# GpSimd normalises the tiles, VectorE keeps their moments

## The reference

```python
def _layernorm(x, axis=-1, eps=1e-05):
    m = jnp.mean(x, axis=axis, keepdims=True)
    v = jnp.var(x, axis=axis, keepdims=True)
    return (x - m) / jnp.sqrt(v + eps)

x = x + self_attention(_layernorm(x))     # layer 0: causal, 16 heads of 16
x = x + cross_attention(_layernorm(x))    # 77 context rows
x = x + experts(_layernorm(x))            # 8 linear experts, top 2
x = x + recurrence(_layernorm(x))         # layer 1: h = tanh(xt + h @ Wh.T + b), 1024 steps
x = x + cross_attention(_layernorm(x))
x = x + gated_experts(_layernorm(x))      # 16 experts in groups, top 4, and a shared one
```

## Time and profile before

| | |
|---|---|
| median of 3 runs | 1412.26 us (1410.08 to 1412.88) |
| the profiled execution, its own time | 1410.35 us |
| its span, first to last instruction | 1408.3 us |
| PE busy | 1353.7 us (96%) |
| DVE busy | 849.8 us (60%) |
| ACT busy | 630.1 us (45%) |
| POOL busy | 39.4 us (3%) |

### The profile page before, as it was taken

How to read it: one execution, slowest core, us unless ns; L and a number is a source line. 1 busy time by engine, 2 the same in 40 slices (tenths; PEclk the granted TensorE clock), 3 DMA queues, 4 the chain that set the end, 5 groups by cost and what they waited for, 6 DMA issues and landing times.

```text
span 1408.3 us, 48623 instructions
## 1 busy us (share of the span) xinstructions
PE 1353.7 (96%) x19876; PEld 918.5 (65%) x19876; DVE 849.8 (60%) x2678; ACT 630.1 (45%) x2842; POOL 39.4 (3%) x60
## 2 busy tenths in 40 slices
PE   4798979999999999999999999999999999999998
PEld 2455436777756777776577777766667776765654
DVE  6757774268775225979661225758555565447585
ACT  2163304833524784253248876553253435433422
POOL 2000000000000000000000000000000000000000
PEclk9899989999999999999999999989999999989999
DMA  5746100021000002110000003310000200001000
GB/s 139 122 124 128 37 1 3 3 50 16 3 2 3 3 3 34 40 34 3 2 3 3 3 3 108 81 30 2 2 2 3 55 3 3 17 3 39 2 16 15
DMA packets 45471, 40.20 MB, mean 29 GB/s; under 512 B 9723, under 2 KB 44486, under 8 KB 45254
## 3 DMA queue, kind: packets, MB, share of 16 engines
q1 hardware_dynamic: 42662, 35.53, 11.1%
q10 hardware_dynamic: 2592, 1.57, 0.9%
HBM read 25.81 MB, written 10.80 MB: 26 GB/s over the span
## 4 chain that ended last, share of the span: by engine, by line
PE 90%; DVE 5%; DMA 1%; ACT 1%; issue 1%; SPq 0%; DVEq 0%; ACTq 0%
PE b L515 23%; PE b L1654 9%; PE b L534 8%; PE b L1431 6%; PE b L1023 6%; PE b L994 5%; PE b L1722 5%; PE b L939 4%; PE b L696 3%; DVE mx L948 3%; PE b L1300 3%; PE b L1275 2%; PE b L744 2%; PE b L459 2%; PE b L651 2%; PE b L501 1%
## 5 line engine op out<-in xcount | busy, mean ns | idle before, releaser
L515 PEld LDWEIGHTS b<-hp,whp 128*128 128x128 f16 x12276 | 472.1, 96 | 255.1 <-ACT hp L560 168.6
L515 PE MATMUL b<-hp,whp 128*128 128x2 f16 x12276 | 532.5, 165 | 1.0
L566 DVE TENSOR_TENSOR hp<-hist,hp 128x4 f16<-128x4 f32 x1023 | 164.5, 161 | 405.6 <-ACT hist L561 394.9
L560 ACT ACTIVATE hp<-b 128x4 f16<-128x4 f32 x1024 | 178.0, 174 | 442.8 <-PE b L515 430.2
L948 DVE TENSOR_REDUCE mx<-b 128x1 f32<-128x512 f32 (+3 forms) x304 | 189.9, 652 | 0.5 <-PE b L939 0.3
L1008 ACT ACTIVATE vp<-b 128x512 f32<-128x512 f32 x288 | 171.7, 603 | 17.7 <-PE b L997 9.8
L561 ACT ACTIVATE hist<-b 128x4 f32<-128x4 f32 x1024 | 177.2, 173 | 0.0
L534 PE MATMUL b<-whp 128*128 128x512 f16 (+6 forms) x608 | 162.1, 342 | 0.0
L1654 PE MATMUL b<-vp,heads 128*128 128x512 f16 x576 | 160.5, 380 | 0.0
L939 PE MATMUL b<-heads 128*128 128x512 f16 (+3 forms) x384 | 113.1, 333 | 5.8 <-DVE mx L948 2.8
L1431 PE MATMUL b<-we,xT 128*128 128x512 f16 x384 | 106.0, 383 | 0.0
(11 more groups left out here) (220 smaller groups left out, 1620.7 us busy)
## 6 DMA issues: line engine op xcount, KB each, us to landing
x_qs<-qx_scr SPq DMA_DIRECT2D x42, 128.0 KB
qx_scr<-xq_pair SPq DMA_DIRECT2D x16, 256.0 KB, 2.1
heads<-q_scr SPq DMA_DIRECT2D x24, 128.0 KB, 5.0
heads<-k_scr SPq DMA_DIRECT2D x36, 64.0 KB, 2.8
x<-in_x SPq DMA_DIRECT2D x8, 256.0 KB, 6.7
q_scr<-tail SPq DMA_DIRECT2D x8, 256.0 KB, 2.3
k_scr<-tail SPq DMA_DIRECT2D x8, 256.0 KB, 2.3
x_qs<-in_L_ffn_We SPq DMA_DIRECT2D x2, 1024.0 KB, 6.2
```

Of the source, the lines that this page charges most:

```text
L515: return pe.matmul(self.z(t)[:, m], self.w.whp[:, a, k, m * P:(m + 1) * P], self.g.hp16[:, (t - 1) % 2, part, k, :], start=False, stop=Tru ...
L560: act.activation(self.g.hp16[:, t % 2, 0], self.z(t), ACT.Tanh, scale=1 / LIFT).then_inc(self.s["hi_ready"], 1)
```

## The change

`normalise` goes from DVE's list to POOL's, with the same instruction, waits and signal. Its cost in the plan becomes 0.75 (it was 0.49), and what follows it sees its signal after 0.15 in the plan (it was 0.06). Moments, power and transposition are as before; the planner makes a new order for all engines from the changed costs.

```diff
         st.add("pool", name + "_power", self.power, n // 2, 0.75, lambda h: rank(2 * h) + 0.4)
-        st.add("v", name + "_normalise", self.normalise, n, 0.49, r(0.5))
+        st.add("pool", name + "_normalise", self.normalise, n, 0.75, r(0.5))
...
-    def normalise(self, v, i):
+    def normalise(self, pool, i):
         t = tile_of(i)[3]
-        v.wait_ge(self.s["power"], i // 2 + 1)
+        pool.wait_ge(self.s["power"], i // 2 + 1)
         if i >= self.ring:
-            v.wait_ge(self.s["turned"], i - self.ring + 1)
-        v.tensor_scalar(self.xn[:, i % self.ring], self.g.x[:, t, :], self.g.mv[:, t, 0:1], self.g.rs[:, t:t + 1],
+            pool.wait_ge(self.s["turned"], i - self.ring + 1)
+        pool.tensor_scalar(self.xn[:, i % self.ring], self.g.x[:, t, :], self.g.mv[:, t, 0:1], self.g.rs[:, t:t + 1],
                         ALU.subtract, ALU.mult).then_inc(self.s["xn"], 1)
```

## The result

| | before | after |
|---|---|---|
| median of 20 runs each | 1410.84 us | 1430.7 us |
| profiled execution, own time | 1410.35 | 1434.52 |
| mean granted clock, profiled execution | 0.977 | 0.963 |
| recurrence, first to last tanh (L560) | 220.2 to 1272.7 | 225.1 to 1296.7 |
| PE idle over the span | 54.6 | 71.0 |

The ratio is 1.0128, with an interval of 1.0104 to 1.0152. I had predicted 1407 us, range 1399 to 1421. The ratios, the medians and the means from here on leave out the slow runs, those over 1.5% above the fastest of the same kernel (two of the 20 after, and one each of before, e5 and e9); without them the median after is 1430.1.

A forecast was written before the change was run, and what follows sets the result against it. DVE was taken to bound about a fifth of the kernel, PE with the recurrence's steps the rest. Terms of 6.6 us faster, zero and 2.0 slower made 4.6 faster: predicted 1407 us, range 1399 to 1421.

The forecast's parts named there:

- the price of POOL's instruction: One normalisation on POOL was taken at 0.55 us, range 0.41 to 1.23, below the planned 0.75.
- fourth rival: Single-buffer groups: above 0.75 us every round is later than planned; at 1.0 us PE loses 5 us, giving 1414; chance 0.08.
- Term 1: Relief of DVE in its full stretches, 32 tiles at 0.33 us: ceiling 10.6 us, taken as 6.6 us faster.
- first rival: Whole ceiling and more: lighter DVE lets the plan drop up to 15.7 us of idle matmuls; 1401, to 1396.6; chance 0.18.
- that shrinking: Sign for the forecast: PE's idle matmuls of L534 fall from 162 us by 5 to 15.
- The halving of the gain beside the recurrence: For 24 tiles beside the recurrence, half the freed DVE time was counted: 4.0 us, bounds 0 and 7.9.
- Term 2: Latency of a tile group: six waiting places 1.5 us slower, shorter DVE queue at the end 1.5 faster, together zero.
- The part that I expected at the end: In n6 of chunk 3 POOL starts the third tile sooner than busy DVE: 1.5 us faster, bounds 0 and 2.7.
- Term 3: POOL and DVE share a port: normalisations beside the recurrence delay DVE's subtraction, 2.0 us slower, bounds 0 and 9.4.
- third rival: POOL's normalisation holds up the recurrence's subtraction L566 for its whole length: slower, 1418 at 0.8 us, 1422 at 0.90; chance 0.21.
- second rival: Nothing moves: PE and the recurrence close up, a new order loses elsewhere what it gains; 1412 us; chance 0.13.
- The signs: Expected: DVE about 38 us lighter, POOL about 90 busy. Wrong if POOL's instruction takes 0.8, steps lengthen or idle matmuls don't shrink.

The follow-up runs named there:

- e5: The changed kernel with a plain copy on POOL in place of the normalisation, mean and factor left out, same order; 1394.7 us, ratio 0.9876.
- e9: The kernel before, normalisation still on DVE, with the factor left out (one arithmetic step); 1409.1 us, ratio 0.9979.
- m1: The kernel before, with nine forms of POOL instruction run twice each after the last store, other engines idle; one execution, no ratio.
- e7: The changed kernel with idle matmuls of 1024 columns before each transposition L459 once the recurrence runs; 1432.2 us, ratio 1.0142.
- e2: The changed kernel's order kept on every engine, but DVE executes the normalisations; 1415.7 us, ratio 1.0017 against before.
- e6: The changed kernel with one arithmetic step on POOL (mean subtracted, factor left out), same order; 1401.0 us, ratio 0.9940.
- e4: The kernel before, plus an unused instruction of the same form on POOL beside each DVE normalisation; 1416.7 us, ratio 1.0045.
- e1: The order of the kernel before kept on every engine, but POOL executes the normalisations; 1456.8 us, ratio 1.0320.
- e10: Against before: tiles of the five single-buffer sublayers split, 128 columns each on POOL and DVE, first sublayer on DVE; 1424.6 us, ratio 1.0081.

## Why the prediction was wrong, step by step

**The step that failed is the price of POOL's instruction.** I chose 0.55 from the row of the same shape; it is 1.24. With it fell what I built on it: "the order has room for it, and PE is not late". The plan had 0.75, and PE was late 42 times, for 20.6 us. The value of the upper bound, 1.23 from a power stretched by a neighbour, was right by accident. The two selections of the earlier trace rows gave 1.2 ns a column; a tensor_scalar with two steps has 3.3. A selection is no measure for arithmetic, and no row of the trace before was a good one; the power's 0.69 for two elements, which I quoted, lay above the price that I chose for 256. The price was unknown between 0.41 and 1.23; I put the forecast, with 0.40 of the chance, near its lower end, and worked out no rival beyond 1.0.

The Trainium skill (GPSIMD Engine Reference, section Performance versus the Vector engine) has elementwise work with two inputs at about twice VectorE's time. For two inputs m1 agrees roughly: 0.72 us on POOL, where DVE's addition of the same shape (L705, one of whose inputs lies in PSUM) took 0.42. For the normalisation, one input and two steps, the factor is three, 1.22 to 0.41; the measurement decides, and my estimate of 0.56 by that page fell with the price.

**The mechanism was the fourth rival's**, with 0.08 the least of my chances: above 0.75 every round of a single buffer is later than planned. I had priced it at one tile in four and 5 us, at d = 1.0. At 1.24 PE waited for 42 of the 80 tiles, 20.6 us (of it 12.2 in 34 waits beside the recurrence). And I had no term for the clock: of the difference of 16.9 us between the means, 9.0 are there at equal clock and 7.9 go with the lower one (0.0084 times 943). How much of that clock is due to the waits is not shown: e7 brought it back by filling them, but e2, with the same order and without them, has 0.9692 too. In e6, at 0.94, PE still waited for POOL 20 times, but 8.7 us in all, and that is less than the relief of DVE is worth. So the sign turns between 0.94 and 1.24.

**Term 1 was too small, and had the instruction been as short as I priced it, the sign would have held.** At equal clock e5 against e2, one order and one plan, differs by 10.5 us for a POOL instruction as long as DVE's own; the ceiling was 10.6 and I took 6.6. The medians differ by 21 us, as e5 has the higher clock too. Against before, e5 at 1394.7 and e6 at 1401.0 gain 17 and 10 us, which is the size of the first rival (1401, down to 1396.6); a right price alone would have left my 4.6 too small. The idle matmuls shrank by 15.8 us even in the kernel that lost (162.1 to 146.3), near the first rival's 15.7. I had named that shrinking as a sign that the forecast works; it is none, because it is made by the plan and not by the chip: e2 has the same 519 of them. The halving of the gain beside the recurrence (no second reduction fits into a step) is the likely weak step in this term; no run tests it by itself.

**Term 2** had six places at 0.14 and 0.1 for the later signal; with 1.24 the same places cost 0.83 each. The start of the recurrence shows it, 225.1 against e2's 219.8 with the same order. The part that I expected at the end seemed to come: from the end of the last variances (L439) to the last transposition of n6 it was 1348.84 - 1343.01 = 5.8 us and is now 1373.31 - 1368.58 = 4.7:

```profile
1368.41 0.17 DVE L439 TENSOR_SCALAR ve<-mv 128x2 f32<-128x2 f32 x1
...
1373.31 0.41 PE L459 MATMUL b<-ident,n_xn 128*128 128x128 f32 x2 [0.52 <-DVE vp L1528]
```

But e2, where DVE still normalises, has 1340.96 - 1337.75 = 3.2 us there:

```profile
1337.58 0.17 DVE L444 TENSOR_SCALAR ve<-mv 128x2 f32<-128x2 f32 x1
...
1340.96 0.38 PE L464 MATMUL b<-ident,n_xn 128*128 128x128 f32 x2
```

So the new order brought 2.6 us and POOL cost 1.5 of them; that my sign came true was luck. (The row after names L1528 as what PE waited for, but POOL's last normalisation ended at 1373.16, 0.12 ahead of the weight load at 1373.28, and in the two rounds before it is 0.11, so POOL held PE as well.)

**Term 3**, the port, 2.0 us slower: about right in size. After the change L566 has a longest of 328 ns, and who waited for it:

```profile
L566 DVE TENSOR_TENSOR hp<-hist,hp x1023: 98/163/328, 225.4 to 1296.0; 128x4 f16<-128x4 f32 x171
...
  PEld b L515: 1.5, 4
  PE b L515: 0.4, 1
```

That is 1.9 us, 1.3 more than the 0.6 before; e4 has 2.6 us at equal clock. During the recurrence 66 subtractions began while POOL was in a normalisation; their median is 0.16 us and the longest took 0.33. **The third rival** gave an outcome of the right sign by the wrong cause: had POOL held the subtraction for its whole 1.24 us, its formula would give 64 x (1.24 - 0.17)²/2.06 = 36 us and subtractions of up to 1.4 us. **The second rival** fell with e1 and e5: the same work but for the normalisation itself, in two orders, lies 62 us apart.

**The signs.** "POOL's instruction takes 0.8 or more" was one of the three by which I would be wrong, and it came; the second, longer steps, came too (1071.6 over 1052.5). DVE's busy time fell by 27.0 us and not by about 38, and POOL's rose to 157.9 and not to about 90.

## What to carry to other kernels

Before work goes to another engine, find a row of that engine with the same operation; an instruction of the same shape but another kind can be off by more than a factor of two, and if there is none, the price's upper end belongs in the forecast. In an order that is written ahead, a planned cost that is too low makes an engine stand in its queue, and everything behind it stands too; here PE held the recurrence, and its clock was lower as well. Correct the plan's price first (here 13.9 us of 18.6), and move only those pieces whose group has room. Before a sign that came true is counted for the idea, run the new order with the old engine (e2): here it had brought the shrinking fillers and the shorter end by itself.

## What the runs showed of the hardware

- POOL runs subtract and multiply over 128x256 float32 in 1.22 us, alone as well as beside a busy DVE (1219 the shortest and 1225 the median in the kernel after); a plain copy takes 0.40.
- POOL is the one that is held up: the longest normalisation after took 2.29 us, and beside it (from 1303.47) DVE ran two instructions L1706 with both inputs in SBUF, from 1303.49 to 1304.84. DVE's small subtraction was never longer than 0.42 (e4), with 1.28 us instructions on POOL beside it. The Trainium skill (SBUF — State Buffer, section Who interferes with whom) speaks of a lock for the whole instruction; the stretched normalisation agrees, but the subtractions don't show one of that length on DVE's side.
- DVE needs 346 ns for 128 columns and 406 for 256 in the same place: splitting a tile there saves next to nothing.
- The granted clock goes with the time by about 9 us for each 0.01 in these kernels. The two in which PE stands most have low means (PE idle over the profiled span 75.9 us and a mean clock of 0.9567 in e1, 71.0 and 0.9684 after, 54.6 and 0.9768 before), but idle time alone does not set it: e2 has 0.9692 and e10 0.9673 at 55.6 and 58.4 us, e6 0.9794 at 57.3.
